# A decoder of four layers in one kernel: early float8 weights, one-variance norms, full-row biases, a third weight slot, causal masks in DVE

## The reference

```
x = x + l0_attn(ln(x))              # 32 heads of 8, rotary, biases in all projections
x = x + ssm(ctx, ln(x))             # selective scan over 256 steps, 16 states
x = x + l0_ffn(ln(x))               # causal attention (32 heads of 64) and 8 experts, below
x = x + l1_attn(ln(x))              # short convolutions, long convolution by Fourier tables
x = x + ssm(ctx, ln(x))
x = x + l1_ffn(ln(x))               # float8 matmuls, below
x = x + l2_attn(ln(x))              # differential: two causal attentions, 32 heads of 8
x = x + l2_cross(ln(x), ctx)
x = x + l2_ffn(ln(x))               # causal attention (32 heads), shared and routed experts
x = x + l3_attn, l3_cross, l3_ffn
```

```python
def ln(x): return (x - mean) / sqrt(var + 1e-5)
def rmsnorm(x, w): return x * rsqrt(mean(x * x) + 1e-5) * w

# l0_ffn, of h0 = ln(x)
h = h0 + attention(rmsnorm(h0, ln1_w), wq, wk, wv, wo)     # causal mask, softmax
t = rmsnorm(h, ln2_w)
probs = softmax(t @ gate_w)                                # 8 experts
topw, topi = top_k(probs, 2); topw = topw / sum(topw)
up = relu(t @ w1[e]) * (t @ w3[e]); out = (up @ w2[e]) * topw     # hidden size 1024

# l1_ffn
def qdot(a, b): return dot(a.astype(float8_e4m3fn), b.astype(float8_e4m3fn), out=bfloat16)
out = qdot(gelu(qdot(x, w_gating[0])) * qdot(x, w_gating[1]), w_linear)

# l2_attn and the attention of l2_ffn
s = q @ k.T * scale + where(lower triangle, 0, -1e30); a = softmax(s)
```

## Time and profile before

| | |
|---|---|
| median of 3 runs | 2655.5 us (2653.11 to 2662.68) |
| profiled execution | 2658.1 us, its span 2656.9 us |
| mean granted TensorE clock | 0.864 of full |
| busy: PE / PEld / DVE / ACT / POOL | 2081.8 / 1444.6 / 1519.9 / 1089.7 / 1048.7 us |
| DMA | 121.38 MB, 46 GB/s on the mean |

### The profile page before, as it was taken

How to read it: one execution, slowest core, us unless ns; L and a number is a source line. 1 busy time by engine, 2 the same in 40 slices (tenths; PEclk the granted TensorE clock), 3 DMA queues, 4 the chain that set the end, 5 groups by cost and what they waited for, 6 DMA issues and landing times. The chain is left out here.

```text
span 2656.9 us, 35337 instructions
## 1 busy us (share of the span) xinstructions
PE 2081.8 (78%) x12705; PEld 1444.6 (54%) x12752; DVE 1519.9 (57%) x2932; ACT 1089.7 (41%) x2195; POOL 1048.7 (39%) x1084
## 2 busy tenths in 40 slices
PE   5667759999956888876524988887999978888887
PEld 2333346667646777763302555445687765555446
DVE  6877655545444555544678655544466554456546
ACT  3245625464523434433166144452343434422433
POOL 2766617455636665650254233341232222322000
PEclk8756679999977999997756978888999989979778
DMA  3222110000014445421001000002000000012000
GB/s 140 72 56 59 49 51 8 23 12 16 5 40 155 149 153 163 147 82 44 9 39 37 2 3 2 3 3 103 1 1 1 1 1 1 3 66 107 2 1 17
DMA packets 49150, 121.38 MB, mean 46 GB/s; under 512 B 5553, under 2 KB 18353, under 8 KB 47185
## 3 DMA queue, kind: packets, MB, share of 16 engines
q1 hardware_dynamic: 47440, 114.92, 13.3%
q0 software_dynamic: 1536, 4.20, 0.5%
HBM read 103.50 MB, written 14.55 MB: 44 GB/s over the span
## 5 line engine op out<-in xcount | busy, mean ns | idle before, releaser
L1796 POOL TENSOR_SCALAR l0f_probs<-l0f_probs,l0f_tot 128x128 f32<-128x128 f32 (+1 forms) x256 | 201.6, 806 | 141.8 <-DVE l0f_tot L1743 141.2
L2018 PE MATMUL ps<-l0f_xh,l0f_wh 128*128 128x256 f32 x480 | 149.3, 311 | 49.6 <-DVE l1x_dBu L649 28.4
L1262 DVE TENSOR_REDUCE l2a_a_max<-ps 128x6 f32<-128x768 f32 x128 | 119.4, 953 | 87.5 <-PE ps L1114 86.9
L3114 POOL TENSOR_TENSOR l2x_probs<-l2x_probs,l2x_rc 128x512 f32<-128x512 f32 x64 | 66.5, 1039 | 254.7 <-DVE l2x_rc L3015 254.7
L1318 POOL TENSOR_SCALAR_AFFINE_SELECT l2a_a_probs<-l2a_a_probs 128x256 f32<-128x256 f32 (+1 forms) x192 | 88.3, 484 | 170.4 <-ACT l2a_a_probs L1224 148.3
L2133 POOL TENSOR_TENSOR l0f_wl<-l0f_raw,l0f_wh 128x1024 fp32r<-128x1024 f32 x60 | 141.8, 2375 | 17.8 <-ACT l0f_wh L2058 17.8
L2019 PE MATMUL ps<-l0f_xl,l0f_wh 128*128 128x256 f32 x480 | 141.0, 294 | 0.0
L2020 PE MATMUL ps<-l0f_xh,l0f_wl 128*128 128x256 f32 x480 | 141.0, 294 | 0.0
L1667 ACT ACTIVATE l0f_probs<-ps,l0f_neg 128x128 f32<-128x128 f32 (+1 forms) x256 | 104.3, 424 | 87.2 <-DVE l0f_neg L1733 87.2
L674 POOL TENSOR_TENSOR l1x_y<-l1x_y,l1x_hc 128x512 f32<-128x512 f32 x64 | 80.8, 1283 | 129.0 <-DVE l1x_hc L665 129.0
L2955 ACT ACTIVATE l2x_probs<-ps,l2x_neg,l2x_rs 128x256 f32<-128x256 f32 x128 | 71.0, 559 | 145.5 <-DVE l2x_neg L3005 145.4
(11 more groups left out here) (728 smaller groups left out, 5858.3 us busy)
## 6 DMA issues: line engine op xcount, KB each, us to landing
l0f_raw<-in_e_l0f SPq DMA_DIRECT2D x60, 512.0 KB, 4.1
l0x_bc<-scratch_bc SPq DMA_DIRECT2D x32, 512.0 KB, 4.8
l0f_raw_d<-in_e_l0f SPq DMA_DIRECT2D x60, 256.0 KB, 3.8
scratch_rows<-zero SPq DMA_DIRECT2D x1, 3840.0 KB, 18.8
l0f_xb<-scratch_rows SPq DMA_DIRECT2D x15, 256.0 KB, 4.5
scratch_results<-l0f_yb SPq DMA_DIRECT2D x15, 256.0 KB, 4.8
l0f_slab<-in_g_l0f SPq DMA_DIRECT2D x8, 448.0 KB, 3.5
l1f_raw<-in_w_l1f SPq DMA_DIRECT2D x1, 3072.0 KB, 9.9
```

The source lines that it names most:

```text
L1262: dve.tensor_reduce(M[:, 2 * half:2 * half + 2, j, :], src.rearrange("p a (c n) -> p a c n", c=NB_), AX.X, ALU.max).then_inc(*unit_max.tick())
L1796: last = pool.tensor_scalar(pr[:, u % 3, a, r], pr[:, u % 3, a, r], tot[:, u % 3, qt, a:a + 1], None, ALU.mult)
L2018: pe.matmul(out, hi, xh[:, j % 2, c, :], start=c == 0, stop=False)
```

## The change

- **Float8 weights early.** `quantise_weights` leaves l1_ffn. A class `Early` loads the same 3 MB in four pieces (on SP, ahead of the Fourier tables) and quantises six chunks in part 1 and six in part 2 of l1_attention; both adds and the subtraction are POOL's. The result, bf16, goes to DRAM (1.5 MB) before the last barrier of that stage's part 2, and l1_ffn loads it back. The turned rows are copied to float8 directly.
- **One-variance norms.** `NormTwice` computes both deviations of l0_ffn and l2_ffn from x's variance, writes xn first, and h behind the turn.
- **Full-row biases.** Bias weights are padded with zeros to 128 rows; the bias product has 128 rows.
- **Three slots** for `wh` and `wl`; ACT cuts two steps ahead; POOL does wl(n) ahead of the scan's add of n − 2.
- **Masks in DVE.** Mask products go; four `tensor_tensor_reduce` per unit add the mask in place (in PSUM) and take the maximum. `kf` has 624 columns, `kb` 512; at the start one cast and one memset remain.
- **Router.** The sum, its reciprocal and the scaling of the probabilities before the top 2 go.

```diff
     dve.tensor_copy(k.kb[:, 0:128], k.ident)
-    dve.tensor_copy(k.kb[:, 128:384], k.kf[:, 368:624])
-    dve.memset(k.kb[:, 384:512], 1.0)
-    dve.tensor_copy(k.kb[:, 512:768], k.kf[:, 624:880])
+    dve.memset(k.kb[:, 128:512], 1.0)
...
+    def masked_max(self, scores, half, out):
+        at = 0 if half else P
+        return self.dve.tensor_tensor_reduce(scores, scores, self.mask[:, at:2 * P], 1.0, 2 * MASKED, ALU.add, ALU.max, out)
...
+class NormTwice:
+    def dve(self):
+        k, dve, v, r = self.k, self.k.dve, self.k.sig("v"), self.r
+        var = k.mv[:, :, 1]
+        dve.tensor_scalar(r[:, 1, :], var, EPS, None, ALU.add).then_inc(*v.tick())
+        dve.wait_ge(*v.now())
+        dve.reciprocal(r[:, 0, :], r[:, 1, :]).then_inc(*v.tick())
+        dve.wait_ge(*v.now())
+        dve.tensor_tensor(r[:, 1, :], r[:, 0, :], var, ALU.mult).then_inc(*v.tick())
+        dve.wait_ge(*v.now())
+        dve.tensor_scalar(r[:, 1, :], r[:, 1, :], EPS, None, ALU.add).then_inc(*v.tick())
+        dve.wait_ge(*v.now())
+        dve.reciprocal(r[:, 1, :], r[:, 1, :]).then_inc(*k.sig("mean_square").tick())
+        dve.wait_ge(*k.sig("root")(1))
+        dve.tensor_tensor(self.both[:, :], r[:, 0, :], r[:, 1, :], ALU.mult).then_inc(*v.tick())
+        dve.wait_ge(*v.now())
+        for i in range(NT):
+            dve.tensor_scalar(self.xn[:, i, :], self.src[:, i, :], k.mv[:, i, 0:1], self.both[:, i:i + 1],
+                              ALU.subtract, ALU.mult).then_inc(*k.sig("normed").tick())
+    def dve_first(self):
+        k = self.k
+        for i in range(NT):
+            k.dve.tensor_scalar(self.h[:, i, :], self.src[:, i, :], k.mv[:, i, 0:1], self.r[:, 0, i:i + 1],
+                                ALU.subtract, ALU.mult).then_inc(*k.sig("v").tick())
...
     if bias is not None:
-        last = k.pe.matmul(out, k.ones[0:1, :], bias, start=False, stop=True)
+        last = k.pe.matmul(out, k.ones, bias, start=False, stop=True)
...
-                if causal:
-                    for a in range(2):
-                        diagonal = banks[:, a, :].rearrange("p (q n) -> p q n", n=S)[:, :, 0:P]
-                        last = pe.matmul(diagonal, k.identb, k.mask_qk.unsqueeze(1).to_broadcast([P, 2, P]), start=False, stop=True)
...
+                if causal:
+                    for a in range(2):
+                        for qt in range(2):
+                            last = k.masked_max(src[:, a, qt * P:P + qt * S], qt, M[:, 2 * half + a, j, qt:qt + 1])
...
-            ln, rn, turn = Norm(k, c2, "l0f_ln", h, k.x), Norm(k, c2, "l0f_rn", xn, h), Turned(k, xT, xn, w["ln1"])
+            norm, turn = NormTwice(k, c2, "l0f_nn", xn, h, k.x), Turned(k, xT, xn, w["ln1"])
...
-                for i, (unit, mask) in enumerate(((k.identb, k.mask_qk), (k.ident_swap, k.mask_swap))):
-                    for r, bank in halves:
-                        diagonal = bank[:, 0:512].rearrange("p (q n) -> p q n", n=S)[:, :, 0:P]
-                        last = pe.matmul(diagonal, unit[r, :], mask[r, :].unsqueeze(1).to_broadcast([64, 2, P]), start=False, stop=i == 1)
...
-                dve.tensor_reduce(m[:, 0, :], banks[:, :, 0:P], AX.X, ALU.max).then_inc(*vc.tick())
-                dve.tensor_reduce(m[:, 1, :], banks[:, :, P:P + S], AX.X, ALU.max).then_inc(*vc.tick())
+                for a in range(2):
+                    for qt in range(2):
+                        k.masked_max(banks[:, a, qt * P:P + qt * S], qt, m[:, qt, a:a + 1]).then_inc(*vc.tick())
...
-        wh, wl = sb("wh", [P, 2, 1024], F32R), sb("wl", [P, 2, 1024], F32R)
+        wh, wl = sb("wh", [P, 3, 1024], F32R), sb("wl", [P, 3, 1024], F32R)
...
-                if n >= 2:
-                    act.wait_ge(*up3(n - 1))
-                act.copy(wh[:, n % 2, :], raw[:, n % 4, :]).then_inc(*w_hi.tick())
+                if n >= 3:
+                    act.wait_ge(*up3(n - 2))
+                act.copy(wh[:, n % 3, :], raw[:, n % 4, :]).then_inc(*w_hi.tick())
...
-                if n + 1 < NS:
-                    cut(n + 1)
+                if n + 2 < NS:
+                    cut(n + 2)
...
-                if n and scan_at(n - 1):
-                    scan.pool(scan_at(n - 1))
+                if n >= 2 and scan_at(n - 2):
+                    scan.pool(scan_at(n - 2))
...
+class Early:
+    CHUNKS, PIECES = 12, ((0, 1), (1, 4), (4, 8), (8, 12))
+    def act(self, i):
+        self.k.act.wait_ge(*self.ready[i])
+        self.quant.act(self.col(self.raw, i), i % 3, i - self.first)
+    def dve(self, i):
+        self.k.dve.wait_ge(*self.ready[i])
+        self.quant.dve_scale(self.col(self.raw, i), i % 3, i - self.first)
+    def pool(self, i):
+        n = i - self.first
+        self.quant.pool_mid(i % 3, n)
+        self.quant.pool_round(self.col(self.raw, i), i % 3, n)
+        self.quant.pool_out(self.col(self.w8, i), i % 3, n)
+    def store(self):
+        self.k.sp.wait_ge(*self.quant.done.now())
+        self.k.sp.dma_start(self.k.kept8, self.w8[:, :]).then_inc(*self.kept.tick())
+        self.k.sp.wait_ge(*self.kept.now())
...
-        k.weights("l1f", "l1f", raw)
+        k.load("l1f", w8[:, :], k.kept8)
-            norm, turn = Norm(k, c2, "l1f_", xn, k.x), Turned(k, xT, xn)
+            norm, turn = Norm(k, c2, "l1f_", xn, k.x), Turned(k, x8, xn, saturate=False)
-            dve.tensor_copy(x8[:, :, :], xT[:, :, :], saturate=False)
-            quantise_weights(k, quant, w8, raw, 6144)
```

More of the change, by code:

```diff
@@ L357, in act @@
             if self.scale is None:
-                k.act.copy(out, k.ps[:, g, :]).then_inc(*xa.tick())
+                k.act.copy(out, k.ps[:, g, :], **self.cast).then_inc(*xa.tick())
             else:
@@ L368, in dve @@
             if self.scale is None:
-                k.dve.tensor_copy(out, k.ps[:, g, :]).then_inc(*xd.tick())
+                k.dve.tensor_copy(out, k.ps[:, g, :], **self.cast).then_inc(*xd.tick())
             else:
@@ L1119, in turn_rows @@
                 pe.wait_ge(*unit_max(NU * (b + 1)))
[L1120 to L1121 removed]
                 pe.wait_ge(*ring_free("rows", b, 0))
                 for qt in range(2):
[L1124 to L1125 removed]
+                    last = pe.transpose(banks[0:H, 0, qt * P:(qt + 1) * P], M[:, :, :, qt], k.ident)
                 last.then_inc(*max_turned.tick())
@@ L1141, in score @@
                         last = pe.matmul(bank[:, i * w:(i + step) * w], KT[z][r, hs.kj(js[i]), kt * P:(kt + 1) * P],
-                                         QT[z][r, js[i]:js[i] + step, q0:q0 + w], start=i == 0, stop=(late or not causal) and i + step == len(js))
-                if causal and not late:
-                    for a in range(2):
-                        diagonal = ps[:, 4 + 2 * (n % 2) + a, :].rearrange("p (j n) -> p j n", n=w)[:, :, 0:P]
-                        last = pe.matmul(diagonal, k.identb, k.mask_kq.unsqueeze(1).to_broadcast([P, len(js), P]), start=False, stop=True)
+                                         QT[z][r, js[i]:js[i] + step, q0:q0 + w], start=i == 0, stop=i + step == len(js))
                 last.then_inc(*scored.tick())
@@ L1260, in largest @@
                     dve.wait_ge(*max_turned(b))
-                src = ring("unit", b, u)[:, :, 0:384] if causal else ring("unit", b, u)
-                dve.tensor_reduce(M[:, 2 * half:2 * half + 2, j, :], src.rearrange("p a (c n) -> p a c n", c=NB_), AX.X, ALU.max).then_inc(*unit_max.tick())
-            def join(b):
-                dve.wait_ge(*unit_max(NU * (b + 1)))
-                dve.tensor_tensor(Mj[:, :, :], M[:, :, :, 1], M[:, :, :, 2], ALU.max).then_inc(*joined.tick())
+                src = ring("unit", b, u)
+                if causal:
+                    for a in range(2):
+                        for qt in range(2):
+                            last = k.masked_max(src[:, a, qt * P:P + qt * S], qt, M[:, 2 * half + a, j, qt:qt + 1])
+                else:
+                    last = dve.tensor_reduce(M[:, 2 * half:2 * half + 2, j, :], src.rearrange("p a (c n) -> p a c n", c=2), AX.X, ALU.max)
+                last.then_inc(*unit_max.tick())
             def split_rows(b):
@@ L1299, in at_dve @@
                     if s == NC - 2:
-                        if causal:
-                            join(it - 1)
                         split_rows(it - 1)
@@ L1494, in l0_ffn @@
             at_dve()
-            ln.act(1)
-            rn.act(2)
+            norm.act()
             turn.act()
-            turn.pe(lambda n: normed(8 + n))
+            turn.pe(k.sig("normed"))
             k.barrier()
@@ L1871, in step @@
             dve.wait_ge(*v.now())
-        dve.tensor_scalar(self.before[:, :], k.kf[:, 368:496], 0.0, None, ALU.is_lt)
+        dve.tensor_scalar(self.before[:, :], k.kf[:, 496:624], 0.0, None, ALU.is_lt)
         src = pr
@@ L1946, in at_dve @@
             dve.wait_ge(*ex(1))
-            dve.tensor_reduce(sm[:, :], pr[:, :, :], AX.X, ALU.add).then_inc(*v.tick())
-            dve.wait_ge(*v.now())
```

(4 more changed lines are left out.)

457 lines of the change are left out of this document (238 added, 219 removed).

## The result

The changed kernel takes 2614.6 us (median, 2613.3 to 2616.7) where the kernel before takes 2654.4 in the same comparison: ratio 0.985, with a 95% interval of 0.983 to 0.987. The forecast was 2540, with a range of 2490 to 2592. A third of the forecast gain came.

What follows compares the result with a forecast made beforehand. TensorE was taken to set the experts and the causal attentions, DVE, ACT and POOL's quantising to delay l1_ffn. The terms summed to −116 us from 2658.1 us profiled (median 2655.5), so about 2540 us, range 2490 to 2592.

Steps and rivals of the forecast that it cites:

- The price: Causal masks: four combined DVE operations take 1.37 us a unit, where one reduce of 768 elements took 0.95.
- side estimate of 1.30 us a unit: Causal masks: DVE's combined operations priced from the skill's errata section; by it l2a would come at −18.
- I let half the units pass the longer reduce on: l2a: half of 128 units pass DVE's extra 0.42 us on to the stage, +27 us.
- TensorE gives back 42: l2a: without mask products TensorE saves 0.33 us in each of 128 units, 42 us; stage taken at −16.
- l2_ffn's attention: Masks in l2f's 32 units: −3 us (−10 to +10).
- the first causal attention: Masks in l0f: −9 us, half of TensorE's 19 at most (−19 to +6).
- Experts: Three slots and POOL's new order remove TensorE's idle time ahead of L2018: −46 us (−30 to −55).
- The rival that another wait would take the place of this one: Experts: scan add, DVE's reading or slabs end last instead of wl, 15 of 46 gained, 2571 us; chance 0.15.
- l1_attention: Quantising moved here: DVE and POOL exclude each other on shared ports, +16.8 us in part 1, +4 in part 2.
- the rival without it: l1_attention part 1 without the DVE-POOL lock: +4 for +16.8 us, whole 2527 us; chance 0.05.
- Biases: Out projections: equal row counts take back 0.27 of 0.66 us a tile, −2.2 us each in l0a and l1a.
- the slower one: Masks: combined operations wait on accumulator writes; from about 2.3 us a unit the kernel is slower, 2695 at 2.5; chance 0.03.

Runs made afterwards that it cites:

- q2: m1 with DVE's reduce cut from 768 to 384 elements per unit in the two small causal attentions: 2544.2 us, 0.956 of before.
- r2: Changed kernel with a reduce of 384 elements and no mask products in the two small causal attentions: 2533.8 us, 0.9535 of before.
- m1: Changed kernel with the old masks (TensorE mask products, one DVE reduce of 768) back in the two small causal attentions: 2554.5 us, 0.962 of before.
- m3: Changed kernel with DVE's old single reduce and no mask in the maximum in the two small causal attentions: 2576.2 us, 0.971 of before.
- q3: m1 with every mask product of the two small causal attentions done twice: 2571.5 us, 0.966 of before.
- m2: Changed kernel keeping DVE's combined operations, with TensorE's mask products put back in the two small causal attentions: 2629.2 us, 0.9885 of before.
- p1: m1 plus one plain DVE reduce of 320 elements per unit in the two small causal attentions: 2640.9 us, 0.9905 of before.
- q4: m1 with four chunks of float8 weights in part 1 of l1_attention and eight in part 2: 2545.4 us, 0.958 of before.
- p4: m1 with two norms in a row and one-row biases again: 2581.5 us, 0.968 of before.
- r3: Changed kernel with old masks in all three causal attentions and four float8 chunks in part 1 of l1_attention: 2546.1 us, 0.959 of before.
- m4: m1 with the old masks of the first causal attention (l0_ffn) back too: 2552.3 us, 0.961 of before.

## Why the prediction was wrong

**The step that failed is the masks in the differential attention**: −42 for TensorE's missing products, +27 for half of DVE's longer list, no term for the granted clock. The stage was to get 16 us shorter and got 53.9 longer. The price of the operation was right. The cases side by side, in us:

| DVE per unit | mask products | l2a | granted clock | TensorE busy | idle |
|---|---|---|---|---|---|
| half a reduce (q2, r2) | on TensorE | 339.8 | 0.80 | 307.2 | 32.6 |
| | none | 318.6 | 0.77 | 260.7 | 57.9 |
| old reduce (m1, m3) | on TensorE | 336.0 | 0.87 | 290.2 | 45.8 |
| | twice (q3) | 360.5 | 0.86 | 322.8 | 37.7 |
| | none | 347.4 | 0.72 | 282.5 | 64.9 |
| combined (m2, after) | on TensorE | 398.1 | 0.71 | 345.3 | 52.8 |
| | none | 387.2 | 0.66 | 304.9 | 82.3 |
| old and 320 elements (p1) | on TensorE | 413.8 | 0.69 | 360.2 | 53.6 |

*The price* was right: 1.37 was taken, and a unit takes about 1.25. Two lines of the kernel before, then groups of the kernel after in l2a by form, and one unit of DVE's timeline:

```profile
1590.97 1.81 DVE L1262 TENSOR_REDUCE l2a_a_max<-ps 128x6 f32<-128x768 f32 x2
L1169 PE MATMUL ps<-kf,l2a_a_oT 128*128 128x128 f32 x128 | 20.7, 285 | 14.7 <-DVE l2a_a_max L1262 11.9 <-ACT l2a_a_oT L1230 2.6
...
L231 DVE CUSTOM_DVE_ANT_0 ps<-ps,kf 128x256 f32<-128x256 f32 x256 | 118.1, 461 | 0.0
L231 DVE CUSTOM_DVE_ANT_0 ps<-ps,kf 128x128 f32<-128x128 f32 x256 | 82.0, 320 | 89.9 <-PE ps L1151 89.8
L231 DVE DVE_READ_ACCUMULATOR2_ANT l2a_a_max<- 128x1 f32 x512 | 70.4, 138 | 0.0
L1151 PE MATMUL ps<-l2a_a_KT,l2a_a_QT 24*128 24x128 f32 x256 | 53.6, 420 | 31.1 <-DVE l2a_a_max L231 21.4 <-ACT l2a_a_QT L1242 5.3 <-ACT l2a_a_KT L1244 2.1
L1200 PE MATMUL ps<-kf,l2a_a_oT 128*128 128x128 f32 x128 | 27.8, 356 | 24.9 <-DVE l2a_a_max L231 22.2 <-ACT l2a_a_oT L1261 2.4
...
1548.27 0.28 DVE L231 CUSTOM_DVE_ANT_0 ps<-ps,kf 128x128 f32<-128x128 f32 x1
1548.48 0.13 DVE L231 DVE_READ_ACCUMULATOR2_ANT l2a_a_max<- 128x1 f32 x1
1548.48 0.46 DVE L231 CUSTOM_DVE_ANT_0 ps<-ps,kf 128x256 f32<-128x256 f32 x1
1548.87 0.13 DVE L231 DVE_READ_ACCUMULATOR2_ANT l2a_a_max<- 128x1 f32 x1
1548.87 0.32 DVE L231 CUSTOM_DVE_ANT_0 ps<-ps,kf 128x128 f32<-128x128 f32 x1
...
1549.49 0.32 DVE L231 CUSTOM_DVE_ANT_0 ps<-ps,kf 128x128 f32<-128x128 f32 x1
```

A main instruction of 128 elements is followed by the next after 0.21 to 0.25 us, one of 256 after 0.39; the accumulator reads exist, one behind each, but the next main instruction starts together with the read, so they cost nothing that shows. The Trainium skill, "VectorE: DVE Perf Modes", section Two Vector instructions with no wait between them, counts two instructions for such an operation, and the trace agrees; it was no reason against the edit. Two old reduces in a row span 1.81 us, 0.95 of it the second's own, so they start 0.86 apart; against that the new list is about +0.40 us a unit. (The prediction's side estimate of 1.30 us a unit would have given −21 for l2a by its own sum, not −18.)

*"I let half the units pass the longer reduce on"* (+27): 0.40×128 = 51 us more of DVE made the stage 62 us longer (m1 to m2), more than all of it. DVE's busy share had misled me: 177 of 333 us looks free, but a PSUM slot of the ring comes back only after DVE has read it, TensorE works its list in order, and behind the waiting product stand all its others. L1151's products (the old L1109) wait 21.4 us for DVE in the group above, where it was 6.1, and L1200's (the old L1169) 22.2 for 11.9. Yet with the same products (m1 to m2) only 7 of the 62 us are TensorE's idle time; 55 are its busy time, at a clock of 0.71 for 0.87. The ring explains that DVE's list matters, not the size.

*"TensorE gives back 42"*: +11 at the old reduce (m3), −11 beside the combined ones (after against m2), −21 beside half a reduce (r2). In all three pairs the kernel without the products has a lower granted clock, a mean between the levels of 2.4 and 1.2 GHz: 0.72 for 0.87, 0.66 for 0.71, 0.77 for 0.80. From m1 to m3 TensorE's busy time fell by 8 us only, though the products that went had 54.7 us of it, and its idle time rose by 19. The clock stood in no term of my sum. What it costs can be estimated from kernels with m1's code in l2a: 336.0 us at 0.87, 339.4 at 0.86 (q4), 343.4 and 343.0 at 0.84 (p4, r3), about 2.5 us for each hundredth. Stretched to m3's 0.15, far outside these readings, that is an estimate of 37 us, most of the 42+11 that are missing. What lowers the clock stays open, and no experiment here isolates it: idle time alone doesn't, as q2 has less of it than m1 (32.6 for 45.8) and the lower clock (0.80 for 0.87).

*Layer 3* got 5.9 us shorter with no edit in it, at a clock of 0.85 for 0.80; over all the kernels here it took 205.7 to 214.4 us with the same code. m1's code took 334 to 343 us in l2a. So a stage of this length moves by some ±5 us which no part of a change explains; in l2a the clock moves with it.

**l2_ffn's attention** failed in the same way (+13.1 for −3; 127.1 in m1, 134.9 in m3, 141.2 in m2), **the first causal attention** more mildly. Its stage grew by 7.7 us, at a clock of 0.95 for 0.98; with the old masks and the new norms (m4) it took 2.2 more than before, with new masks and old norms (p4) 4.0 more. By m4 and r3 the masks are worth nothing there that stands out of the spread of 396.5 to 402.0 us, and not −9.

**Experts**: the mechanism was right, POOL's order ahead of TensorE's start; the term was too small, −58.5 for −46. I had counted only L2018's idle time. Besides, TensorE's busy time in the two windows fell from 292.8/57 = 5.14 us a step to 256.1/51.4 = 4.98 as the clock rose from 0.97 to 1.00: (5.96−5.06)×60 = 54, and 4 us lie outside the loop. The share between slot and order, on which the prediction said nothing, is 15 to 44. The rival that another wait would take the place of this one is refuted (0.1 us left).

**l1_attention**: the lock is real, the rival without it is out. DVE and POOL in part 1 of the kernel after:

```profile
1174.74 2.17 DVE L2470 TENSOR_TENSOR l1a_kv<-l1a_kv,l1a_v 128x1024 f32<-128x1024 f32 x1
1190.67 1.23 DVE L2470 TENSOR_TENSOR l1a_kv<-l1a_kv,l1a_v 128x1024 f32<-128x1024 f32 x1
...
1155.28 1.27 POOL L2351 TENSOR_TENSOR l1f_early_M<-l1f_early_M,l1f_early_I 128x512 f32<-128x512 f32 x1 [8.87 <-ACT l1f_early_I L2322]
1173.70 2.13 POOL L2359 TENSOR_TENSOR l1f_early_w<-l1f_early_I,l1f_early_M 128x512 bf16<-128x512 f32 x1
1187.43 2.12 POOL L2359 TENSOR_TENSOR l1f_early_w<-l1f_early_I,l1f_early_M 128x512 bf16<-128x512 f32 x1
...
1192.22 1.09 PE L2495 MATMUL ps<-kf,l1a_kv 128*128 128x128 f32 x4 [18.11 <-PEq L239]
```

The same tensor_tensor takes 2.17 us beside POOL's (at 1174.74, POOL's until 1175.83) and 1.23 when POOL is through (1190.67, POOL's last ended at 1189.55), and POOL's own goes from 1.27 to 2.13. By the Trainium skill, "SBUF — State Buffer", section Who interferes with whom, a VectorE instruction with two SBUF inputs and a GpSimd one that reads SBUF exclude each other; by that rule, the trace agrees. TensorE pays, with 18.1 us of idling ahead of part 2's first product, where it was 6.7 before. Size: DVE's part 1 takes from its first norm row to its end 44.9 us for 33.4, +11.5 and not +16.8; POOL was idle there for 8.9 and 2.7 us at a time, which my hand-made schedule had not, and which is the likely reason. Part 2 came at +4.6, as taken: 13.0−11.5, with the biases' −3.1 taken out.

**Biases**: tiles of l1_attention's out projection on TensorE:

```profile
1247.77 1.03 PE L437 MATMUL ps<-w_l1a,l1a_kv 128*128 128x256 f32 x4
1249.06 1.03 PE L437 MATMUL ps<-w_l1a,l1a_kv 128*128 128x256 f32 x4
```

1.29 us a tile for 1.68, −0.39 where −0.27 was taken, of the 0.66 that the two gaps had. **Start**, **l1_ffn**, **norms** and **router** came as forecast, within 1 us; l0_attention brought 3 us more than its biases were given, and p4 puts 4.3 us there down to them.

**The rivals**: the slower one had the right place, DVE's list in l2a, and the wrong lever. It asked for 2.3 us a unit before the kernel would be slower than before; in fact 1.25 made the masks lose 62 us against the old ones (after against m4), because I let DVE's list cost time only once it was as long as the stage, and had no price for the clock. The whole is faster only because experts and l1_ffn bring 58.5+43.9 = 102.

## What to carry to other kernels

An engine that is busy for half of a stage can still set it, if it empties a ring of two slots for an engine that works in order: lengthen its piece by a plain filler, or halve it, and read what the stage does, before trusting the busy share. Work taken from TensorE brought at most half of its time here, and once a loss; look at the granted clock of the stage, and at how TensorE's time splits into busy and idle, and count a lower clock among the costs. And before adding a buffer, look at the order of the queue that fills it: here the order was worth 44 us, the buffer alone nothing.
